# Cross-attention and a recurrent feed-forward layer in float32: the softmax reciprocals brought into the attention's layout by a small VectorE turn and transfers through memory, in place of TensorE transposes

## What is computed

```python
def attn(q, ctx):                        # 16 heads of width 32
    scores = q @ ctx.T / sqrt(32)        # -inf where |i - j| > 64
    return softmax(scores) @ ctx @ W_proj.T + b_proj
x = x + attn(layernorm(x), ctx)
xn = layernorm(x)
for xt in xn:                            # over the 8 batch entries
    c = sigmoid(f(xt, c)) * c + sigmoid(i(xt, c)) * tanh(g(xt, c))
out = x + tanh(xn @ Wo.T + c @ Uo.T + bo)
```

## Time and profile before

| | us |
|---|---|
| median of 3 runs | 1018.29 |
| lowest, highest | 1018.28, 1021.04 |
| profiled execution | 1014.17 |
| its span in the trace | 1012.4 |
| PE busy | 986.0 |
| DVE busy | 605.5 |
| ACT busy | 500.8 |
| POOL busy | 226.8 |

### The profile page before, as it was taken

How to read it: one execution, slowest core, us unless ns; L and a number is a source line. 1 busy time by engine, 2 the same in 40 slices (tenths; PEclk the granted TensorE clock), 3 DMA queues, 4 the chain that set the end, 5 groups by cost and what they waited for, 6 DMA issues and landing times.

```text
span 1012.4 us, 20358 instructions
## 1 busy us (share of the span) xinstructions
PE 986.0 (97%) x7100; PEld 748.4 (74%) x7100; DVE 605.5 (60%) x2194; ACT 500.8 (49%) x1472; POOL 226.8 (22%) x320
## 2 busy tenths in 40 slices
PE   6998999999999999999999999999999999999997
PEld 4664567777777777777777777777777778888886
DVE  5676887776567755776677656775586532133222
ACT  5767666555555445555455545455455432131221
POOL 4555322211111111211111111111121110002354
PEclk9998999999999999999999999999999999999999
DMA  8355322222222222211222222111111012029666
GB/s 268 123 153 177 110 74 79 84 79 74 80 84 79 74 70 67 71 46 63 78 85 80 73 80 84 58 53 48 61 38 50 11 39 108 0 99 360 247 218 198
DMA packets 76245, 99.37 MB, mean 98 GB/s; under 512 B 5232, under 2 KB 46192, under 8 KB 74608
## 3 DMA queue, kind: packets, MB, share of 16 engines
q1 hardware_dynamic: 75424, 97.80, 30.2%
q10 hardware_dynamic: 720, 0.27, 0.1%
HBM read 68.69 MB, written 29.36 MB: 97 GB/s over the span
## 4 chain that ended last, share of the span: by engine, by line
PE 87%; DMA 5%; DVE 2%; ACT 2%; issue 2%; POOL 1%; SPq 1%; DVEq 0%; POOLq 0%; ACTq 0%
PE ps_g L494 18%; PE ps_g L496 16%; PE ps_g L495 16%; PE ps_a L530 7%; PE ps_a L549 4%; PE ps_v L570 3%; PE ps_m L494 3%; PE ps_m L496 3%; PE ps_m L495 3%; PE ps_m L592 2%; PE ps_v L575 2%; ACT probs L670 1%; PE ps_m L604 1%; DMA keys<-x_dram 1%; PE ps_m L505 1%
## 5 line engine op out<-in xcount | busy, mean ns | idle before, releaser
L767 DVE CUSTOM_DVE_ANT_0 probs<-ps_a,mask 128x192 f32<-128x192 f32 (+1 forms) x512 | 169.5, 387 | 167.8 <-PE ps_a L530 158.8
L670 ACT ACTIVATE probs<-probs,rowmin 128x192 f32<-128x192 f32 (+1 forms) x512 | 239.2, 473 | 1.6 <-DVE rowmin L767 1.6
L712 ACT ACTIVATE gate<-ps_g,bias 128x512 f32<-128x512 f32 x84 | 57.8, 688 | 211.4 <-PE ps_g L496 211.4
L790 DVE STREAM_TRANSPOSE probs_t<-probs 32x128 f32<-32x128 f32 x492 | 146.5, 298 | 6.0
L478 POOL COPY recip<-invsum 128x128 f32<-128x128 f32 x128 | 37.7, 295 | 488.1 <-DVE invsum L774 488.1
L494 PE MATMUL ps_g<-state_hi,gate_w 128*128 128x512 f32 x336 | 138.2, 411 | 0.0
L675 ACT ACTIVATE probs_t<-ps_a 128x512 f32<-128x512 f32 x108 | 64.4, 596 | 147.4 <-PE ps_a L549 146.8
L496 PE MATMUL ps_g<-state_hi,gate_w 128*128 128x512 f32 x336 | 131.4, 391 | 0.0
L495 PE MATMUL ps_g<-state_lo,gate_w 128*128 128x512 f32 x336 | 131.3, 391 | 0.0
L670 ACT ACTIVATION_READ_ACCUMULATOR probs<-probs,rowmin 128x1 f32 x512 | 98.8, 193 | 0.0
L530 PE MATMUL ps_a<-keys,queries 32*128 32x256 f32 (+1 forms) x1024 | 86.2, 407 | 2.1 <-DVE rowmin L767 1.3
(11 more groups left out here) (177 smaller groups left out, 1764.6 us busy)
## 6 DMA issues: line engine op xcount, KB each, us to landing
values<-ctx_rows SPq DMA_DIRECT2D x34, 256.0 KB, 4.3
xr<-x SPq DMA_DIRECT2D x32, 256.0 KB, 3.9
keys<-ctx_t SPq DMA_DIRECT2D x16, 512.0 KB, 4.1
x_dram<-xr SPq DMA_DIRECT2D x32, 256.0 KB, 4.2
gate_w<-x2t_dram SPq DMA_DIRECT2D x8, 1024.0 KB, 10.9
keys<-ctx_t SPq DMA_DIRECT2D x16, 384.0 KB, 3.4
x2t_dram<-x2t_even SPq DMA_DIRECT2D x12, 512.0 KB, 4.0
x2t_dram<-x2t_odd SPq DMA_DIRECT2D x12, 512.0 KB, 3.8
```

Source lines behind the costliest of these rows:

```text
L670: act.activation(row, row, ACT.Exp, bias=rowmin[:, i % 2, h:h + 1], scale=-1.0, accum_out=rowsum[:, i // G % 2, i % G, h:h + 1]).then_inc( ...
L712: act.activation(gate[:, min(gt, 1), :], ps_g[i % 2][:, :], ACT.Tanh, bias=(first_bias if b == 0 else bias)[:, gt, m:m + 1], scale=1.0 if ...
L767: dve.tensor_tensor_reduce(probs[:, i % 2, h, 0:SEEN[t]], ps_a[h][:, 0:SEEN[t]], mask[:, MASK0[t]:MASK0[t] + SEEN[t]], -SCALE, -NEG, ALU.a ...
L790: turn = dve.transpose(probs_t[BLK * keys_of:BLK * (keys_of + 1), HPG:2 * HPG, q], probs[q, i % 2, :, col:col + BLK])
```

## The change

`recip`, POOL's copies, PE's `spread` and ACT's copy (L478, L584, L679) go. In their place:

- DVE writes the reciprocals of a tile side by side into `invsum`, 128 rows by 16 columns (in a 32-column tile whose rest is zero).
- Twice per tile a new step `spread` turns `invsum` by one DVE instruction in 32x32 blocks into `invsum_t`: part 0 after the reciprocals of the tile's third slot, part 1 after those of the fourth. Both turns are of all 32 columns.
- For each part SP writes `invsum_t` to a scratch tensor in memory (16 KB), waits until that has landed, and issues four reads that bring the reciprocals back, each repeated over 32 partitions, into `recip`: three of the four groups in part 0 (4 x 48 KB), the last in part 1 (4 x 16 KB).
- DVE's second turn writes the same `invsum_t`, so it waits until the first write has landed (`recip_sent`).
- `mult` now multiplies `ps_v` by `recip` and waits for both parts (`recip_in`) and for the PE turns that last read `tile_row`.
- In tiles 0 to 4 `mult` moves from the end of the tile's fourth slot into the next slot, behind that slot's `turn` step.

```diff
+        if s == 0 and n <= OWN_BANKS:
+            tile_steps("mult", i - 1)
...
-            tile_steps(("proj", "query", "turn2", "spread")[s], (i - 1, i + 1, i - 1, i)[s])
+            tile_steps(("proj", "query", "turn2", None)[s], (i - 1, i + 1, i - 1, -1)[s])
...
             steps.append(("recip", n + 1))
+            if (n + 1) % G == G - 2:
+                steps.append(("spread", 2 * ((n + 1) // G)))
+            if (n + 1) % G == G - 1:
+                steps.append(("spread", 2 * ((n + 1) // G) + 1))
...
-        if s == 3 and early:
-            tile_steps("mult", i)
...
+                if kind == "spread":
+                    tile, part = i // 2, i % 2
+                    first, last = (0, G - 1) if part == 0 else (G - 1, G)
+                    sp.wait_ge(inv_turned, i + 1)
+                    sp.dma_start(recip_dram[i].rearrange("c (a j) -> a c j", j=HEAD), invsum_t[:, :])\
+                      .then_inc(recip_sent, DMA)
+                    sp.wait_ge(recip_sent, DMA * (i + 1))
+                    need(sp, attn_t, tile)
+                    rows = recip_dram[i, 0:HPG * G, :].rearrange("(h g) q -> h g q", h=HPG)[:, first:last, :]
+                    for h in range(HPG):
+                        sp.dma_start(recip[HEAD * h:HEAD * (h + 1), first:last, :],
+                                     rows[h:h + 1].to_broadcast([HEAD, last - first, P])).then_inc(recip_in, DMA)
...
-                if kind == "spread":
-                    pe.wait_ge(inv, G * (i + 1))
+                if kind == "proj":
                     need(pe, q_ready, min(i + 2, TILES))
                     need(pe, x2_lo, i)
-                    for g in range(G):
-                        mm = pe.transpose(ps_m[:, g * P:(g + 1) * P], recip[:, g, :], ident[:, :])
-                    mm.then_inc(spread, 1)
...
+                if kind == "spread":
+                    tile, part = i // 2, i % 2
+                    dve.wait_ge(inverted, G * tile + G - 1 + part)
+                    need(dve, recip_sent, DMA * i)
+                    dve.transpose(invsum_t[:, :], invsum[:, :]).then_inc(inv_turned, 1)
...
                 if kind == "mult":
-                    dve.wait_ge(recip_out, i + 1)
+                    dve.wait_ge(recip_in, 2 * HPG * DMA * (i + 1))
                     dve.wait_ge(valued, G * (i + 1))
-                    dve.tensor_tensor(tile_row[:, :], ps_v[:, :], tile_row[:, :], ALU.mult).then_inc(attn_t, 1)
+                    dve.wait_ge(q_turned, min(i + 2, TILES))
+                    need(dve, x2_turned, i)
+                    dve.tensor_tensor(tile_row[:, :], ps_v[:, :], recip[:, :, :].rearrange("p g q -> p (g q)"),
+                                      ALU.mult).then_inc(attn_t, 1)
```

More of the change, by code:

```diff
@@ L21, in bass_xattn_ffn @@
 def bass_xattn_ffn(nc, x, ctx_rows, ctx_t, w_proj, b_proj, w_gates, u_gates, biases, w_out, u_out, b_out, in_c,
-                   out, x1_dram, x2t_dram):
+                   out, x1_dram, x2t_dram, recip_dram):
     B, T, D = x.shape
@@ L148, in bass_xattn_ffn @@
             if s > 0:
-                tile_steps((None, "query", "turn2", "spread")[s], (None, i + 1, i - 1, i)[s])
+                tile_steps((None, "query", "turn2", None)[s], (None, i + 1, i - 1, -1)[s])
             cells(2)
@@ L257, in bass_xattn_ffn @@
         rowsum = sb("rowsum", [P, 2, G, HPG], F32)
-        invsum = sb("invsum", [P, 2, G, HPG], F32)
+        invsum = sb("invsum", [P, HEAD], F32)
+        inv_rows = invsum[:, 0:HPG * G].rearrange("p (h g) -> p h g", h=HPG)
+        invsum_t = sb("invsum_t", [P, HEAD], F32)
         bias = sb("bias", [P, NG, G], F32)
@@ L263, in bass_xattn_ffn @@
         st1 = sb("st1", [P, 2, 6], F32)
-        mv1 = sb("mv1", [P, 2, 2], F32)
-        ve1 = sb("ve1", [P, 2], F32)
-        rs1 = sb("rs1", [P, 2], F32)
         st2 = sb("st2", [P, 2, 6], F32)
-        mv2 = sb("mv2", [P, 2, 2], F32)
-        ve2 = sb("ve2", [P, 2], F32)
-        rs2 = sb("rs2", [P, 2], F32)
+        moments = sb("moments", [P, 4, 4], F32)
+        mv1, mv2 = [moments[:, a, :].rearrange("p (r m) -> p r m", r=2) for a in range(2)]
+        ve1, rs1 = moments[:, 2, 0:2], moments[:, 2, 2:4]
+        ve2, rs2 = moments[:, 3, 0:2], moments[:, 3, 2:4]
         ps_a = [pb(f"ps_a{h}") for h in range(HPG)]
@@ L284, in bass_xattn_ffn @@
         x2t_out = [sem("x2t_out0"), sem("x2t_out1")]
+        recip_sent = sem("recip_sent"); recip_in = sem("recip_in")
         raw_in = sem("raw_in"); bo_in = sem("bo_in")
@@ L290, in bass_xattn_ffn @@
         consts = sem("consts"); rstd1 = sem("rstd1"); rstd2 = sem("rstd2"); xr_ready = sem("xr_ready")
[L291 removed]
+        w_lo = sem("w_lo"); summed = sem("summed")
         attn_split = sem("attn_split"); wp_lo = sem("wp_lo")
         stat1 = sem("stat1"); aggr1 = sem("aggr1"); var1 = sem("var1"); ln1 = sem("ln1")
[L295 removed]
+        masked = sem("masked"); inverted = sem("inverted"); inv_turned = sem("inv_turned"); padded = sem("padded"); turned_b = sem("turned_b"); cleared = sem("cleared")
         attn_t = sem("attn_t"); x1_done = sem("x1_done")
@@ L300, in bass_xattn_ffn @@
         out_lo = sem("out_lo"); emptied_ps = sem("emptied_ps"); last_summed = sem("last_summed")
-        q_ready = sem("q_ready"); expd = sem("expd"); turned_a = sem("turned_a"); recip_out = sem("recip_out")
+        q_ready = sem("q_ready"); expd = sem("expd"); turned_a = sem("turned_a");
         attn_round = sem("attn_round"); wp_hi = sem("wp_hi")
@@ L307, in bass_xattn_ffn @@
         q_turned = sem("q_turned"); scored = sem("scored"); turned = sem("turned"); turned_2 = sem("turned_2"); valued = sem("valued")
-        spread = sem("spread"); projected = sem("projected"); state_used = sem("state_used")
+        projected = sem("projected"); state_used = sem("state_used")
         column = sem("column")
@@ L474, in _ @@
                         .then_inc(attn_split, 1)
[L475 to L480, removed]
                 if kind == "stat2":
@@ L676, in _ @@
                        .then_inc(turned_a, 1)
-                if kind == "spread":
-                    act.wait_ge(spread, i + 1)
-                    act.activation(attn, ps_m[:, :].rearrange("p (g q) -> p g q", g=G), ACT.Copy).then_inc(recip_out, 1)
                 if kind == "halves":
@@ L731, in _ @@
         def _(dve):
+            dve.memset(invsum[:, :], 0.0).then_inc(padded, 1)
             dve.wait_ge(consts, 6)
@@ L772, in _ @@
                     dve.wait_ge(expd, HPG * (i + 1))
-                    need(dve, inv, i - 2 * G + 1)
-                    dve.reciprocal(invsum[:, r, g, :], rowsum[:, r, g, :]).then_inc(inverted, 1)
+                    if i == 0:
+                        dve.wait_ge(padded, 1)
+                    need(dve, inv_turned, 2 * (i // G) + (g == G - 1))
+                    dve.reciprocal(inv_rows[:, :, g], rowsum[:, r, g, :]).then_inc(inverted, 1)
+                if kind == "spread":
[3 more added lines that the diff above has]
+                    dve.transpose(invsum_t[:, :], invsum[:, :]).then_inc(inv_turned, 1)
                 if kind == "turn" and i < OWN_BANKS:
@@ L912 @@
     B, T, D = arrays["x"].shape
+    recip_dram = nc.dram_tensor("recip_dram", (2 * B * T // P, HEAD, P), F32, kind="Internal").ap()
     x2t_dram = nc.dram_tensor("x2t_dram", (B, P, 2, D // P, T), F32, kind="Internal").ap()
@@ L915 @@
                    [d["w_c"], d["w_i"], d["w_f"]], [d["u_c"], d["u_i"], d["u_f"]],
-                   [d["b_c"], d["b_i"], d["b_f"]], d["w_out"], d["u_out"], d["b_out"], d["in_c"], out, x1_dram, x2t_dram)
+                   [d["b_c"], d["b_i"], d["b_f"]], d["w_out"], d["u_out"], d["b_out"], d["in_c"], out, x1_dram, x2t_dram,
+                   recip_dram)
     r = run_bass_kernel_spmd(nc, [arrays], core_ids=[0])
```

1 line of the change is left out of this document (removed).

## The result

The changed kernel takes 1081.88 us (median of 4 runs, 1079.59 to 1083.65) against 1018.28: a ratio of 1.061, 95% interval 1.058 to 1.064. It is slower by 6%. The forecast was 1056 with a range of 1014 to 1086, so the direction and the mechanism held and the size was too small. The profiled execution is 1083.3 us, its span 1081.5.

The account below looks back on a forecast made before the run. PE was taken to bound the long stage; removed transposes against late chains summed to +39.5 us on the profiled 1014.2, or 1054, and 1058 by the runs' median. The forecast taken was 1056 us, range 1014 to 1086.

Parts of the forecast that it names:

- The bound and the gain: PE, without idle in the long stage, gains 0.44 us per tile from the removed transposes, 14 us at most.
- The chain: Last reciprocal to `mult`: turn, write landed, four issues, last read landed; at least 5.5 us, 8.4 in tile 16.
- A small write behind the large one: In SP's queue, part 0's write lands only after the `x1` rows, part 1's only after the 512 KB write.
- The long stage: Tiles 9 to 31: 1 us for tiles 9 to 11, 10.5 for 12 to 23, -2 for 24 to 31.
- Tiles 5 to 8: Chains of 7.5 to 8.4 us against 4.5 to 5.4 of room, 12 us lost in all.
- the rule that each us beyond the room costs one us: Each tile changes by chain minus room where positive; any wait of PE is time lost one for one.
- the room: How late after the last reciprocal `mult` may come before PE waits: 6.2 us in tile 16, 4.6 in tile 6.
- Tiles 0 to 4: Chains of about 10, 12, 13, 10 and 9 us, 26 us beyond the room, counted as 18.
- That discount: In tiles 0 to 4 delays overlap and PE and ACT idle time absorbs part, so two thirds of 26 us, 18.
- Rival 1: The chain of transfers is short, since 16 KB is little and DMA is 25% busy: 1009 us, chance 0.16.
- Rival 2: SP's waits for landings delay weight chunks of slots 4 to 17, 15 to 20 us on top: 1075, chance 0.09.
- Rival 3: No change, because `mult`'s delay falls where PE waits anyway: 1018 us, chance 0.07.

Follow-up runs that it names:

- e_order: The changed kernel, with SP issuing each part's write of the reciprocals ahead of the two large writes (`x1` rows, turned second normalization): 1044.1 us.
- e_late: Tiles 0 to 8 spread the reciprocals the old way (copies and transposes), tiles 9 to 31 as in the changed kernel: 1029.3 us.
- e_early: Tiles 0 to 8 as in the changed kernel, tiles 9 to 31 the old way (copies and transposes): 1066.5 us.
- e_free: The changed kernel with all its transfers, but the multiplication does not wait for them and uses a constant tile: 1013.5 us.
- e_both: Tiles 0 to 8 the old way, tiles 9 to 31 as in the changed kernel with SP's two large writes moved behind the part's reads: 1011.3 us.
- e_both1: e_both with one read of 128 partitions in place of four of 32, for part 1 only: 1007.1 us.
- e_behind: The changed kernel in all tiles, with SP's two large writes moved behind the part's reads: 1044.5 us.

## Why the prediction was right, and where it was too small

**The bound and the gain** held. The transposes are worth 0.44 us a tile in the long stage and 13.6 us in all (1018.3 to 1004.7), as 14 had been the most.

**The chain** held in its parts. A small write behind the large one was the assumption on which all rested, and e_order shows it for part 1 and the 512 KB. For part 0 I had named the wrong transfer: putting the `x1` rows behind it changed nothing in e_order. For tile 16 I had 8.4 us and it is 7.4. The `x1` rows landed after 4.1 us rather than 5.3, and part 0's reads went 3.0 us after its write where I had 4.9; part 1's write took 3.9 rather than 3.4. For tiles 0 to 4 I had 10, 12, 13, 10 and 9 us; from reciprocal to `mult` they took 8.0, 10.5, 13.3, 11.0 and 8.3. For tiles 5 to 8 I had 7.5 to 8.4; they took 9.1, 8.0, 8.5 and 8.7.

**The long stage** (tiles 9 to 31) I had at +9.5 us; the trace has +11.0 and e_late 11 (interval 5 to 16). That the sum is so near is partly luck: tiles 9 to 11 I had at 1 and they lost 3.0, tiles 12 to 23 at 10.5 and they lost 8.6, tiles 24 to 31 at -2 and they have -0.6.

**Tiles 5 to 8** I had at +12, and they lost 23.3. By the measured chains they are 15 us late. The step that failed is the rule that each us beyond the room costs one us: 15 us late cost 23.3. Each wait of 3.6 to 5.0 us is followed by 6 to 7 us at half clock, which undoes up to 3 us of PE's work; over four tiles that is more than the missing 8. But it was not measured apart, and DVE, nearly full in two of these stretches, is a rival for a part of it; what the surplus of 8 us is made of stays open.

**Tiles 0 to 4** I had at 26, of which I took two thirds, 18; they lost 34 by the trace. (By medians the two early groups together lost 48 in e_early, where I had 30.) That discount was the mis-sized term. The reason I gave for it, idle time that takes up a part, was wrong in sign: by the measured chains they are 22 us late, up to 9 us come on top through late weights (e_free), and the clock again (granted 0.73 to 0.89 between 52 and 141 us). How the last two share their part stays open, and so does how much of the 34 is the spread of this group.

**The rivals.** Rival 1, the short chain, had -9 us for the long stage. With no large write ahead e_both has -6.5 there and e_both1 -9.6, so in that stage it was wrong on the queue and not on the price. For tiles 0 to 8 it was wrong on both: e_behind has the same order in all tiles and still loses 38 us there. Rival 2, SP itself, is real, but 9 us at most and not 15 to 20, and the smaller part. Rival 3 falls with e_late: in a stage without idle nothing was taken up.

## What to carry to other kernels

Cost a chain of transfers by what stands ahead of it in its queue, not by its bytes. Here a write of 16 KB took 2.0 us alone and, in the long stage, mostly 3.3 and up to 3.9 behind 512 KB; putting the small urgent write first was worth 38 us with no other change. Compare it with the room tile by tile, and use it only in the stages that have it. In all tiles the change lost 64 us, in tiles 9 to 31 alone still 11; it won 11 us only in tiles 9 to 31, with the large writes behind the reads and part 1 read in one piece. And a wait of several us can cost more than itself: in tiles 5 to 8 chains that were 15 us late cost 23.

## What the runs showed of the hardware that I had not expected

- After a wait of 4.15 us in tile 6 the granted clock was 0.50 for some 6 us, nearly all of them full work. Shorter waits can do it too: in tile 12, after two of 0.84 and 1.27 us close together, it fell once more (row below). Elsewhere from 310 to 700 us, where PE's waits are 1.3 us at most, it stayed at 1.00.

```profile
367.00:371.00 4.00, 3.30 (x21) 2.48 (x22) 3.77 (x16) 1.04 (x4) 0.00 (x0) 0.58 0.00 0
```

- A repeated read of 192 KB in one transfer, with a 512 KB write issued 0.6 us behind it, made that write land after 6.5 us; as four reads of 48 KB issued over 1.9 us, 3.6. Only four of the write's 16 semaphore updates were late, which points to a read that went through four DMA engines.
- In e_both about every third tile from tile 10 on (10, 13, 16, 19, 22, 25, 28) had its last read land late. In tile 13 it took 3.0 us where the others of that part took 1.7 to 2.1, and in that stretch the profile has an instruction fetch on queue q8.

```profile
328.59 1.70 SPq L424 DMA_DIRECT2D recip<-recip_dram  x4
...
recip<-recip_dram SPq DMA_DIRECT2D x1, 16.0 KB, 3.0
...
q8 instruction: 1, 0.02, 1.3%
```

The traces of the changed kernel, e_order and e_both from 240 us on have 548 such reads. 59 took longer than 2.45 us (a bound set after looking at them), and every one of them had an instruction fetch (q8 or q14) begin between 1 us before its issue and its landing; of the 489 others 142 had. That goes well beyond chance, but that the fetch is the cause was not tested.
